# Five coefficient-times-state products moved from VectorE to GpSimd, in front of GpSimd's adding DMA

## The reference

```
h = s0; h0 = s0
for _ in range(5):
    prev = h
    h = D * (c0*h0 - 2*E*h + cm_x*roll(h, 1, W) + cp_x*roll(h, -1, W)
                           + cm_y*roll(h, 1, C) + cp_y*roll(h, -1, C))
    h = h + D*(2*DT)*s0
    h0 = prev
```

## Time and profile before

| | |
|---|---|
| Median of 3 runs | 284.3 us (283.94 to 284.4) |
| Profiled execution, its own time | 284.37 us |
| Its span (first to last instruction) | 282.6 us |
| VectorE (DVE) busy | 251.6 us, 89% |
| TensorE (PE) busy | 235.3 us, 83% |
| ScalarE (ACT) busy | 130.0 us, 46% |
| GpSimd (POOL) busy | 15.9 us, 6% |

### The profile page before, as it was taken

How to read it: one execution, slowest core, us unless ns; L and a number is a source line. 1 busy time by engine, 2 the same in 40 slices (tenths; PEclk the granted TensorE clock), 3 DMA queues, 4 the chain that set the end, 5 groups by cost and what they waited for, 6 DMA issues and landing times.

```text
span 282.6 us, 5201 instructions
## 1 busy us (share of the span) xinstructions
PE 235.3 (83%) x2264; PEld 210.7 (75%) x2264; DVE 251.6 (89%) x199; ACT 130.0 (46%) x202; POOL 15.9 (6%) x35
## 2 busy tenths in 40 slices
PE   0137999999759998279999999999999876699793
PEld 0136899889725597279999999898989776688682
DVE  3899999999999979999999999999999978986820
ACT  3295678876973204602723516061420515336743
POOL 2000000003300101111000101010101000000000
PEclk9999999999968999959999999999999999979999
DMA  7950000007992701990700425176700040000123
GB/s 201 345 118 0 0 6 3 2 0 148 205 207 43 148 0 37 203 204 3 151 0 2 93 58 111 39 174 125 148 3 1 0 147 3 2 0 0 45 106 148
DMA packets 6758, 22.84 MB, mean 81 GB/s; under 512 B 2768, under 2 KB 3024, under 8 KB 4944
## 3 DMA queue, kind: packets, MB, share of 16 engines
q0 software_dynamic: 2160, 13.63, 24.2%
q1 hardware_dynamic: 4432, 8.56, 9.9%
q10 hardware_dynamic: 144, 0.33, 0.4%
HBM read 6.79 MB, written 2.10 MB: 31 GB/s over the span
## 4 chain that ended last, share of the span: by engine, by line
DVE 49%; PE 36%; issue 8%; ACT 4%; DMA 1%; DVEq 0%; ACTq 0%
DVE ring L897 22%; PE psum L1155 16%; DVE coef L637 8%; PE psum L1233 7%; PE psum L1145 7%; PE psum L1062 3%; DVE first_two L980 3%; DVE coef L940 2%; PE psum L1092 2%; ACT coef L370 2%; DVE lo_s L721 2%; DVE state L713 2%; DVE ring L706 1%; DMA bn<-in_norms 1%; DVE hi_s L718 1%
## 5 line engine op out<-in xcount | busy, mean ns | idle before, releaser
L897 DVE TENSOR_TENSOR ring<-coef,state 128x2048 f32<-128x2048 f32 x51 | 113.4, 2286 | 2.7 <-PE psum L1155 2.5
L1155 PE MATMUL psum<-mats,ring 128*128 128x128 f32 x816 | 97.7, 280 | 13.8 <-DVE ring L897 13.8
L1155 PEld LDWEIGHTS psum<-mats,ring 128*128 128x128 f32 x816 | 92.5, 145 | 17.2 <-DVE ring L897 16.7
L370 ACT ACTIVATE state<-psum 128x1024 f32<-128x1024 f32 x36 | 35.1, 1029 | 83.9 <-PE psum L1155 70.1
L637 DVE SCALAR_TENSOR_TENSOR coef<-coef 128x2048 f32<-128x2048 f32 x16 | 36.6, 2290 | 0.5
L1114 PEld LDWEIGHTS psum<-coef,state 32*128 32x128 f32 x672 | 19.4, 187 | 1.7 <-issue 1.7
L1114 PE MATMUL psum<-coef,state 32*128 32x64 f32 x672 | 20.1, 271 | 0.2 <-issue 0.2
L1233 PE MATMUL psum<-hi,dense_m 128*128 128x512 f32 x48 | 20.0, 417 | 0.0
L370 ACT ACTIVATE coef<-psum 128x512 f32<-128x512 f32 (+1 forms) x22 | 17.3, 791 | 5.7 <-PE psum L1092 4.3
L1233 PE MATMUL psum<-lo,dense_m 128*128 128x512 f32 x48 | 19.3, 403 | 0.0
L1155 PE MATMUL psum<-mats,first_two 128*128 128x128 f32 x144 | 17.2, 273 | 1.2 <-ACT state L370 1.2
(11 more groups left out here) (132 smaller groups left out, 277.3 us busy)
## 6 DMA issues: line engine op xcount, KB each, us to landing
first_two<-coef POOLq DMA_DIRECT2D x7, 1024.0 KB, 7.3
coef<-coef POOLq DMA_DIRECT2D x4, 1024.0 KB, 9.0
coef<-in_x SPq DMA_DIRECT2D x2, 1024.0 KB, 7.2
coef<-in_wide_taps SPq DMA_DIRECT2D x3, 384.0 KB, 8.0
ring<-in_x SPq DMA_DIRECT2D x2, 512.0 KB, 6.1
ring<-in_x SPq DMA_DIRECT2D x1, 1024.0 KB, 11.2
out<-coef SPq DMA_DIRECT2D x2, 512.0 KB, 3.1
out<-coef SPq DMA_DIRECT2D x4, 256.0 KB, 2.4
```

Source lines behind the costliest of these rows:

```text
L370: return nc.scalar.activation(dst, src, func, **kw)
L897: V.tensor_tensor(wc(ring[:, slot, :]), wc(coef[:, t, a, :]), h_at(t, k, dw, dc), ALU.mult)\
L1155: ins = mm(slot_ap(name)[:, (j % 8) * 128:(j % 8) * 128 + 128], src[:, j * 128:j * 128 + 128], ident, is_transpose=True, start=first and j ...
```

## The change

The product A0 * h is taken out of VectorE's `step` and is issued by GpSimd in its loop over the tile-steps, directly in front of its own adding DMA. GpSimd waits first for `halo_ready` (the state of the step is complete) and `kept_free[t]`; its wait for `kept_made[t]`, now raised by itself, stays. The condition picks the same five tile-steps. Nothing else changes.

```diff
             for k, t in ORDER:
                 if k and kept(k + 1, t) and k + 1 < STEPS:
+                    pool.wait_ge(halo_ready, 4 * states_through(k - 1, t))
+                    pool.wait_ge(kept_free[t], k)
+                    nc.gpsimd.tensor_tensor(wc(first_two[t][:, :]), wc(coef[:, t, A0, :]), h_at(t, k), ALU.mult)\
+                        .then_inc(kept_made[t], 1)
                     pool.wait_ge(kept_made[t], k)
                     pool.wait_ge(source_scaled, t + 1)
                     pool.dma_start(first_two[t][:, :], coef[:, t, FS, :], accum_op=ALU.add).then_inc(kept_full[t], 16)
@@ VectorE, step(k, t) @@
                     multiply(t, k, a, dw, dc)
                     then(i)
-                if k and k + 1 < STEPS and kept(k + 1, t):
-                    dve.wait_ge(kept_free[t], k)
-                    V.tensor_tensor(wc(first_two[t][:, :]), wc(coef[:, t, A0, :]), h_at(t, k), ALU.mult)\
-                        .then_inc(kept_made[t], 1)
```

## The result

The changed kernel takes 294.92 us (median of four runs, 294.44 to 295.27) against 284.21 us for the kernel before in the same comparison: a ratio of 1.0383, with a 95% interval of 1.0366 to 1.0400. It is slower by 10.7 us; the forecast was 295.2. The profiled execution took 295.13 us with a span of 293.0.

A forecast was written before the change was run, and what follows sets the result against it. VectorE and TensorE lie close together, VectorE setting the pace in several tile-steps; five products at + 2.3 us give + 11.5, less a 0.7 pause: 284.37 + 10.8 = 295.2 us, whole range 284 to 304.

The forecast's parts named there:

- The full stop: Beside each GpSimd product VectorE does nothing for its whole 4.5 us; chance 0.70, range 290 to 304 us.
- the free neighbour: Rival: GpSimd reads beside VectorE without disturbing it, TensorE becomes the bound; 280.9 us, chance 0.14.
- GpSimd's duration: Each two-input GpSimd product of 128x2048: 4.5 us, between 3.6 for two passes and 5.4 for three.
- The even sum: Each of five tile-steps with a kept product goes from 13.2 to 15.5 us on VectorE: + 2.3 each, + 11.5.
- part on what is removed: Five VectorE products go, 11.0 us; without replacement 3.5 us gained, nothing from (1,0), where TensorE is full behind it.
- The pause of 0.69 us: VectorE's wait for TensorE in (2,0) goes, as TensorE catches up while VectorE stands: - 0.7 us.
- The clock: TensorE's granted clock may fall in gaps: counted at zero, without cover up to 5 x 1.1 = 5.5 us.
- the 4 us gap: A stop early in a tile-step leaves TensorE without products for some 4 us.
- Latency: Moved product and adding DMA land before TensorE wants them, 11 to 12 us to spare in (2,0) and (3,0); cost nothing.

The follow-up runs named there:

- The first: Changed kernel with GpSimd filling the kept term with zeros by memset instead of making the product: 281.12 us, ratio 0.9891 to the kernel before.
- second: Changed kernel with GpSimd copying A0 into the kept term instead of multiplying by the state: 282.24 us, ratio 0.9940 to the kernel before.
- last experiments: Changed kernel with VectorE multiplying by constant 0.5 instead of the state in five tile-steps: 283.87 us, single run, against 283.70 for the kernel before.
- the product of (1,0) alone: Changed kernel with GpSimd making only tile-step (1,0)'s product, VectorE the other four: 286.68 us, ratio 1.0104 to the kernel before.
- all but (1,0): Changed kernel with VectorE keeping tile-step (1,0)'s product, GpSimd making the other four: 290.61 us, ratio 1.0234 to the kernel before.
- the four pieces: Changed kernel with each GpSimd product cut into four instructions of 512 columns: 292.54 us, ratio 1.0305 to the kernel before.

## Why the prediction was right

**The mechanism.** The full stop was chosen over the free neighbour because the two-input product takes twice the one-input copy. That was an inference from durations; the runs bear the stop out: reading stops VectorE, writing doesn't, and the loss goes with the columns read. They don't bear out the reason as far as it made the second input special: the one-input form of 1.23 us was stopped too. The Trainium skill, page "SBUF — State Buffer", section "Who interferes with whom", says that a GpSimd instruction that only writes doesn't contend with a two-input VectorE instruction and that VectorE's fast one-input form can contend with GpSimd. The first, second and last experiments agree with it (no loss beside the memset, 1.7 us beside the copy, 0.69 us for the one-input form), the last on a small clash only.

**GpSimd's duration.** 4.5 us was taken as the middle of two and three passes; alone it is 4.2, less than the 4497 ns quoted beside the estimate, and 4.53 with a product of VectorE to let pass first. But what counts for VectorE is 4.0 (4.54 less some 0.5 during which VectorE's product before it was still ending). Here the size was off: + 1.8 for a tile-step with VectorE setting the pace, not + 2.3. The table has it: 15.02 us against the 15.5 worked out.

**The even sum.** "Five of them + 11.5" was wrong for (1,0). The prediction's own part on what is removed says that TensorE is full behind that product, so its removal gives nothing; the sum then credited it with 2.2 us all the same. It cost 4.6 us in the profile, 3.1 by the stop and, by comparison with a second profile, some 1.5 by the clock. In return the mark of (3,1) came 0.99 us nearer: with no kept product between (2,1) and (4,0) VectorE was no longer late there, a gain that the sum had left out. The errors nearly cancel: 4 x 1.8 in place of 4 x 2.3 is - 2.0; (1,0) is + 4.6 in place of + 2.3, + 2.3; (2,0) and (1,1) are 0.6 and 0.4 more, as the old pace in them was partly TensorE's; (3,1) - 1.0. With the 0.1 of (2,0) that makes the table's 11.8 in place of 11.5; less the 0.4 of an earlier start and the 1.0 regained at the end, 10.4 us of span against the 10.8 forecast. So that 295.2 came within 0.3 us of the measured time is luck; the stop and its rough size were not.

**The pause of 0.69 us** did not go: VectorE paused 1.05 us in (2,0), of which GpSimd used the whole, and 2.00 us in (0,1), behind a TensorE made late by the stop and by its clock (0.76 us with the product of (1,0) alone, where the clock was back earlier).

**The clock** was counted at zero with a bound of 1.1 us for each tile-step. In the profile of the changed kernel it was low in (1,0) alone. In the other four, TensorE's longest wait was 1.7 us and the granted clock stayed at 1.00. That was not sure to be so: in the profile of all but (1,0) it did fall, behind a wait of 2.13 us in (2,0), and TensorE's slack didn't cover all of it in that tile-step. But the 4 us gap that I had feared isn't there, since TensorE has the state's and the kept term's transposes and two or three ring products before it when the stop begins.

**Latency.** Right: the adding DMA was issued at 171.41, 186.43 and 201.47, and TensorE never waited for a DMA in this stage. Even with the four pieces spanning 12 us there was room: the DMA behind them is issued 0.3 us after 190.58, would land by that page's median of 7.2 us at 198.1, and is wanted at 206.39.

## What to carry to other kernels

Moving a float32 elementwise product from a full VectorE to an idle GpSimd does not unload VectorE when both read from the on-chip memory: price the GpSimd instruction at its reading time *on VectorE* (here 2.0 ns a column against 1.1 saved). It can pay for instructions that only write, or where VectorE pauses anyway. A copy is a poor candidate here: on GpSimd it took 1.7 us from VectorE, which makes one itself in 1.23. And in a sum over like steps, ask of each step which engine set its pace before: to take the same product from VectorE was worth nothing in (1,0) and a microsecond where VectorE set the pace.

## What the runs showed of the hardware that was not expected

- VectorE and GpSimd take turns after each instruction, in both directions, when both have more to read, with no fixed price that could be seen: losses of 1.0, 2.0 and 4.0 us for 512, 1024 and 2048 columns.
- A GpSimd copy of 128x2048 (1.9 to 2.3 us) cost VectorE 1.7 us, and a GpSimd memset of the same size (1.82 us) nothing.
- VectorE's one-input instruction of 1.23 us, too, was held up beside a reading GpSimd product: it began 0.84 us before the product's end and took 0.69 us longer.
- How long TensorE stayed at 1.2 GHz behind the same wait of 6.4 us varied from one profile to another (back at 2.4 GHz at about 125.1 us in one, at about 133.6 in another with the same work until then). The two groups of times 2.5 us apart out of one kernel differ in mean granted clock (0.967 and 0.955); that it was this stretch which parted them is not shown.
